# Cross-attention of 64 batches on one core: third q projection moved, residual on ScalarE and GpSimd, value spread reshaped

## What is computed

```python
q = split_heads(x @ w_q)                       # 20 heads of 16
out_text = merge(softmax(q @ k.T / 4) @ v)     # 69 keys
out_ip   = merge(softmax(q @ k_ip.T / 4 + mask) @ v_ip)   # 8 keys
out = (out_text + out_ip) @ w_out + b_out + x  # b_out + x: "the residual"
```

## Time and profile before

| what | us |
|---|---|
| median of 3 runs (1338.42 to 1345.62) | 1341.73 |
| the profiled execution | 1338.48 |
| its span on the core | 1336.7 |
| TensorE busy | 1191.8 (89%) |
| VectorE busy | 1094.9 (82%) |
| ScalarE busy | 833.2 (62%) |
| GpSimd busy | 824.0 (62%) |

### The profile page before, as it was taken

The page is one execution under the profiler, slowest core; times in us unless marked ns, Lnnn a source line. Parts: engine busy times, 40 slices in busy tenths (PEclk is TensorE's granted clock), DMA queues, the critical chain, the costliest instruction groups (busy, mean ns, idle before and its releaser), DMA issues.

```text
span 1336.7 us, 33739 instructions
## 1 busy us (share of the span) xinstructions
PE 1191.8 (89%) x12350; PEld 1113.1 (83%) x12350; DVE 1094.9 (82%) x2438; ACT 833.2 (62%) x1795; POOL 824.0 (62%) x1004
## 2 busy tenths in 40 slices
PE   6998885389999999999999999999999999999986
PEld 5898875278888888888888888888888888888885
DVE  4688876268888888888888888888888888888884
ACT  3343444167777777777667767777777777777761
POOL 0111010057777777777777777777777777777774
PEclk9999998589999999999999999999999999999997
DMA  6388888534444444444444444444454444444431
GB/s 163 68 203 159 182 150 132 97 83 110 110 108 108 108 108 109 109 108 110 107 110 110 111 109 109 108 112 112 110 120 114 112 113 109 108 107 108 97 75 40
DMA packets 361459, 151.26 MB, mean 113 GB/s; under 512 B 298641, under 2 KB 350865, under 8 KB 360017
## 3 DMA queue, kind: packets, MB, share of 16 engines
q1 hardware_dynamic: 361296, 149.13, 50.2%
HBM read 88.17 MB, written 39.90 MB: 96 GB/s over the span
## 4 chain that ended last, share of the span: by engine, by line
DVE 33%; PE 33%; issue 7%; ACT 6%; POOL 1%; DVEq 0%; DMA 0%; POOLq 0%; SPq 0%; ACTq 0%
DVE q_hi_lo L1204 8%; DVE stats L1217 8%; PE ps_a L963 7%; PE ps_b L963 7%; DVE values L1261 6%; PE ps_o L1037 5%; PE ps_m L982 4%; ACT q_hi_lo L1134 4%; DVE y L1251 3%; DVE aT_lo L1238 3%; PE ps_s L1006 3%; PE ps_s L1012 3%; PE ps_a L1055 3%; DVE aT L1240 2%; DVE ip_masked L1214 2%
## 5 line engine op out<-in xcount | busy, mean ns | idle before, releaser
L1318 POOL TENSOR_TENSOR prob_lo<-prob,prob_hi 128x512 f16<-128x512 f32 (+1 forms) x448 | 488.9, 1097 | 181.3 <-ACT prob_hi L1154 174.7
L1153 ACT ACTIVATE prob<-ps_s 128x512 f32<-128x512 f32 (+1 forms) x448 | 254.9, 569 | 249.0 <-PE ps_s L1012 248.6
L1006 PE MATMUL ps_s<-q_hi_lo,keys 128*128 128x256 f32 x960 | 256.5, 304 | 0.0
L1154 ACT ACTIVATE prob_hi<-ps_s 128x512 f16<-128x512 f32 (+1 forms) x448 | 252.3, 563 | 0.0
L1012 PE MATMUL ps_s<-q_hi_extra,keys 128*128 128x256 f32 x960 | 234.4, 281 | 0.7 <-ACT q_hi_extra L1143 0.7
L1217 DVE TENSOR_REDUCE stats<-ps_m 128x8 f32<-128x552 f32 x320 | 230.6, 721 | 0.0
L1327 POOL TENSOR_TENSOR attn<-heads 128x128 f32<-128x128 f32 (+1 forms) x256 | 158.4, 619 | 72.9 <-DVE heads L1231 72.8
L1037 PE MATMUL ps_o<-values,prob_hi 128*128 128x68 f16 (+7 forms) x3328 | 197.2, 195 | 3.6 <-DVE heads L1231 1.9
L1037 PEld LDWEIGHTS ps_o<-values,prob_hi 128*128 128x128 f16 x3328 | 168.5, 98 | 24.3 <-DVE heads L1231 2.2
L1037 PE MATMUL ps_o<-values,prob_lo 128*128 128x68 f16 (+3 forms) x1664 | 188.1, 195 | 0.0
L1012 PEld LDWEIGHTS ps_s<-q_hi_extra,keys 128*128 128x128 f32 x960 | 173.0, 189 | 0.9 <-ACT q_hi_extra L1143 0.9
(11 more groups left out here) (179 smaller groups left out, 3094.9 us busy)
## 6 DMA issues: line engine op xcount, KB each, us to landing
x_in<-in_x_dram SPq DMA_DIRECT2D x64, 320.0 KB, 3.0
q_hi_extra<-q_hi_lo SPq DMA_DIRECT2D x64, 320.0 KB, 3.3
x_keep<-in_x_dram SPq DMA_DIRECT2D x64, 320.0 KB, 4.1
out_dram<-y SPq DMA_DIRECT2D x128, 160.0 KB, 2.9
k_scratch<-k_stage SPq DMA_DIRECT2D x16, 770.0 KB, 5.7
keys<-k_scratch SPq DMA_DIRECT2D x256, 48.1 KB, 2.1
ctx_in<-in_ctx_dram SPq DMA_DIRECT2D x64, 128.0 KB, 2.8
keys<-k_scratch SPq DMA_DIRECT2D x256, 24.1 KB, 1.9
```

What stands on the lines that cost most here:

```text
L1006: mm(ps, keys[:, n, 0, quad, c:c + P], q_hl[n][:, quad, :], start=i == 0, stop=False)
L1153: nc.scalar.activation(prob[:, s, 0:w], ps_s[RING[s]][:, 0:w], ACT.Exp)
L1154: nc.scalar.activation(prob_hi[par(b)][:, s, 0:w], ps_s[RING[s]][:, 0:w], ACT.Exp).then_inc(s_hi, 1)
L1318: nc.gpsimd.tensor_tensor(prob_lo[par(b)][:, s, 0:w], prob[:, s, 0:w], prob_hi[par(b)][:, s, 0:w], ALU.subtract).then_inc(s_lo, 1)
```

## The change

Three things change.

- The third q projection writes `ps_a` instead of `ps_b`. It moves ahead of `stats_transpose`, which now writes `ps_b`. On ScalarE `q_hi(2)` moves ahead of `extra`. On TensorE `max_scores(a,0)` moves ahead of `scores(b,0)`.
- `finish(t)` is split. ScalarE copies the output projection to `y` (`y_out`, ahead of `exps(2)` and `exps(3)`), GpSimd adds `x_keep` in place, both tiles after `rest(4)`. TensorE waits for ScalarE's copies (`s_ye`) before it writes the banks again; the stores wait for GpSimd's (`s_yr`).
- The spread writes four slots of each tile. The fifth slot is used by tiles 1, 6 and 11 alone; one more instruction of 3 x 32 elements, behind the third spread, writes these three.

```diff
+MAIN_SLOTS = 4
+WIDE = [t for t, n in enumerate(NSLOTS) if n > MAIN_SLOTS]
 # SyncE, load_values
-                            sp.wait_ge(s_vx, at(b, 3, 3))
+                            sp.wait_ge(s_vx, at(b, 4, 4))
 # TensorE: x_transpose (attn_transpose: the same change of semaphore)
-                            pe.wait_ge(s_yr, at(b, NT, -3 * NT))
+                            pe.wait_ge(s_ye, at(b, NT, -3 * NT))
 # project
-                            pe.wait_ge(s_qlo, at(b, QUADS, 4))
-                        ps = (ps_a, ps_b, ps_b)[m]
+                            pe.wait_ge(s_qlo, at(b, QUADS, 2))
+                        ps = (ps_a, ps_b, ps_a)[m]
 # stats_transpose
-                            pe.wait_ge(s_qlo, at(b, QUADS, QUADS + 2))
+                            pe.wait_ge(s_qlo, at(b, QUADS, QUADS + 4))
-                            last = nc.tensor.transpose(ps_a[:, t * P:(t + 1) * P], stats[:, t, :], ident[:])
+                            last = nc.tensor.transpose(ps_b[:, t * P:(t + 1) * P], stats[:, t, :], ident[:])
 # TensorE's step
-                        if Bs:
-                            scores(b, 0)
                         if A:
                             max_scores(a, 0)
+                        if Bs:
+                            scores(b, 0)
...
+                        if E:
+                            project(e, 2)
                         if A:
                             stats_transpose(a, E, Ds)
-                        if E:
-                            project(e, 2)
 # ScalarE
+                        def y_out(t):
+                            act.wait_ge(s_op, at(d, NT, t + 1))
+                            if t == 0 and (n is None or n >= 4):
+                                act.wait_ge(s_y[par(d)], nth(d, 32, -32))
+                            nc.scalar.copy(y[par(d)][:, t, :], (ps_a, ps_b)[t][:, 0:D]).then_inc(s_ye, 1)
 # VectorE: finish() and its two calls are gone; in spread_values
-                                .broadcast_to([P, GTILES[g], SLOTS, 2 * DH]),
-                                own_rows[:].rearrange("p t (n c) -> p t n c", n=SLOTS)[:, t], ALU.mult).then_inc(s_vx, 1)
+                                .broadcast_to([P, GTILES[g], MAIN_SLOTS, 2 * DH]),
+                                own[:, t, 0:MAIN_SLOTS, :], ALU.mult).then_inc(s_vx, 1)
+                            if g == 2:
+                                w = slice(WIDE[0], TILES, 5)
+                                nc.vector.tensor_tensor(v[:, w, MAIN_SLOTS, 2:SLOT], raw_v[par(b)][:, w, :],
+                                                        own[:, w, MAIN_SLOTS, :], ALU.mult).then_inc(s_vx, 1)
 # GpSimd
+                        def finish(t):
+                            pool.wait_ge(s_ye, at(d, NT, t + 1))
+                            if t == 0:
+                                pool.wait_ge(s_xb, at(d, 1, 1))
+                            nc.gpsimd.tensor_tensor(y[par(d)][:, t, :], y[par(d)][:, t, :], x_keep[par(d)][:, t, :],
+                                                    ALU.add).then_inc(s_yr, 1)
...
                             rest(3)
                             rest(4)
+                        if Ds:
+                            finish(0)
+                            finish(1)
                         if Cs:
                             add_heads(2)
```

More of the change, by code:

```diff
@@ L89 @@
 SLOTS = max(NSLOTS)
+MAIN_SLOTS = 4
+WIDE = [t for t, n in enumerate(NSLOTS) if n > MAIN_SLOTS]
+assert SLOTS == MAIN_SLOTS + 1 and WIDE == list(range(WIDE[0], TILES, 5))
 VCOLS = TILES * SLOTS * SLOT
@@ L824, in xattn_kernel @@
             s_yr = sem("y_ready")
+            s_ye = sem("y_evacuated")
             s_xk = [sem(f"residual_loaded{q}") for q in range(2)]
@@ L1019, in sum_heads @@
                         if u == 0:
-                            pe.wait_ge(s_vx, at(b, 3, 3))
+                            pe.wait_ge(s_vx, at(b, 4, 4))
                         if t == 0:
@@ L1050, in attn_transpose @@
                         else:
-                            wait(pe, s_yr, b, NT, 0)
+                            wait(pe, s_ye, b, NT, 0)
                         for t in range(NT):
@@ L1068, in step @@
                         e, a, c, d = off(b, 2), off(b, 1), off(b, -1), off(b, -2)
+                        if A:
+                            max_scores(a, 0)
                         if Bs:
                             scores(b, 0)
-                        if A:
-                            max_scores(a, 0)
                         if Cs:
@@ L1139, in a_hi @@
                             nc.scalar.copy(aT2[0:64, :], ps_b[0:64, 0:S]).then_inc(s_ahi, 1)
+                        def y_out(t):
[3 more added lines that the diff above has]
+                            nc.scalar.copy(y[par(d)][:, t, :], (ps_a, ps_b)[t][:, 0:D]).then_inc(s_ye, 1)
                         def extra():
                             act.wait_ge(s_et, at(a, 1, 1))
-                            nc.scalar.copy(q_ex[par(a)][QD:P, 0, :], ps_a[QD:P, 0:S]).then_inc(s_ex, 1)
+                            nc.scalar.copy(q_ex[par(a)][QD:P, 0, :], ps_b[QD:P, 0:S]).then_inc(s_ex, 1)
                             nc.scalar.copy(q_ex[par(a)][QD:P, 1:QUADS, :],
-                                           ps_a[QD:P, 0:S].rearrange("p (o s) -> p o s", o=1).broadcast_to([QD, QUADS - 1, S])
+                                           ps_b[QD:P, 0:S].rearrange("p (o s) -> p o s", o=1).broadcast_to([QD, QUADS - 1, S])
                                            ).then_inc(s_ex, 1)
@@ L1162, in step @@
                             exps(1)
+                        if Ds:
+                            y_out(0)
+                        if Bs:
                             exps(2)
+                        if Ds:
+                            y_out(1)
+                        if Bs:
                             exps(3)
@@ L1174, in step @@
                             exps(6)
+                        if E:
+                            q_hi(2)
                         if A:
                             extra()
-                        if E:
-                            q_hi(2)
                     sched(act, step)
@@ L1241, in a_lo @@
                                                     ALU.subtract).then_inc(s_alo, 1)
[L1243 to L1252, removed]
                         def spread_values(g):
@@ L1312, in step @@
                         E, A, Bs, Cs, Ds = has(n)
-                        a, c = off(b, 1), off(b, -1)
+                        a, c, d = off(b, 1), off(b, -1), off(b, -2)
                         def rest(s):
```

9 lines of the change are left out of this document (3 added, 6 removed).

## The result

The changed kernel takes 1344.32 us (median of 9 runs, 1342.9 to 1347.51), the one before 1339.61 in the runs beside it (9 runs, 1338.42 to 1345.62). The ratio is 1.0034, with a 95% interval of 1.002 to 1.0049. Forecast was 1337.5, a little faster.

A forecast was written before the change was run, and what follows sets the result against it. TensorE's chain with ScalarE and VectorE was taken to bound the 16.34 us step; after the change, GpSimd or `q_lo(2)`. 60 steps x -0.11 = -6.6, edges +3, rounded to -4: 1334.5 profiled, 1337.5 median; range 1324 to 1354.

The forecast's parts named there:

- What bounds the kernel: One 16.34 us step: no engine has much room; the chain runs over TensorE, ScalarE and VectorE, GpSimd not on it.
- X to P: From the start of `attn_transpose` to the next step's `project(e,0)`: 10.10 us, claimed unchanged on this path.
- P to X: From the start of `project(e,0)` to that of `attn_transpose`: 6.24 us, claimed to become 5.9.
- Part 1: Third projection: TensorE's wait before `project(e,2)` goes, a 0.26 wait for `extra` replaces it; -0.34 a step.
- Part 2: Residual: ScalarE's copies at 0.43 each cost nothing, GpSimd's two additions take 1.66 against 1.81 of slack.
- GpSimd's sum: GpSimd's instructions from `rest(2)` through `add_heads(3)`, added up: next `attn_transpose` 16.12 to 16.15 after the last.
- Part 3: Smaller spreads save GpSimd 0.1 a step; the small spread waits for `add_heads(3)` (16.35) or not (16.13); middle 16.23.
- rival 3: The small spread hands the whole gain back: step 16.35, with +3 at the ends 1345; chance 0.23.
- Edges: First and last steps: GpSimd's additions +3.1 in two late steps, very end +0.9, first three steps -1; together +3.
- The signs: Expected in traces: GpSimd without idle from `rest(2)` to `add_heads(3)`, small spread 0.6 if waiting, VectorE -6 points, GpSimd +10.
- Rival 1: GpSimd is not the limit, additions 0.75 each; TensorE's path gives step 16.00, -18 us, 1324; chance 0.15.
- rival 2: Slower by GpSimd alone: additions 0.93 each and the small spread waits; step 16.55, +17 us, 1359; chance 0.20.

## Why the prediction was wrong

Point by point, by its own steps.

- **What bounds the kernel.** Right. From X to P it is 10.10 in the changed kernel too. The part alone that shortens P to X gave 18 us. In every run but two it stays at 10.10 to 10.13; where the small spread held up `maxima(3)` it took 11.40, and with `a_hi` ahead of `exps(0)` 10.60.
- **Part 1** was costed at -0.34 a step and measured -0.23 by itself. The wait for `extra` was forecast at 0.26 with TensorE going on at P + 4.93; the changed kernel shows 0.22 and P + 5.05, the projection alone 0.23 and P + 5.03. That tenth is the miss: from there to X the projection alone takes 0.97, as forecast, and X to P does not change.
- **Part 2** in full steps: right, 0.43 a copy, 0.86 an addition (0.87 forecast), and hidden, by the run with the residual alone.
- **GpSimd's sum.** Right within 0.1: 16.12 to 16.15 forecast, 16.13 in the run with the small spread in the middle. That run does not single it out: `attn_transpose` starts 0.09 after GpSimd's last addition there, and so it does in the projection alone (16.12), where GpSimd has pauses and TensorE's own path sets X. With five slots (16.25) the sum is what is left. Its own prices moved against each other. The second spread ran ahead of `rest(2)`, because VectorE was free earlier, so `rest(2)` took 1.40 and the bias addition 1.56, where I had the delay on the bias.
- **Part 3 is the step that failed.** The two ends were 16.13 and 16.35, by whether the small spread waits for `add_heads(3)`. I took the middle, for which there was no row, though the earlier trace rows showed on VectorE's side that the waiting operation goes before the next one of the engine that runs. Read the other way round it says that GpSimd's waiting instruction goes before VectorE's next. It does: in each run that has a small spread, it ended with the same GpSimd instruction in 61 or 62 of its 64 executions. This was rival 3, put at 0.23, which gave 1345, and 1344.32 was measured. In terms of the sum: 16.23 was taken, 16.40 measured, and 60 times 0.17 is 10 us of the miss in the profiled execution.
- **A waiter was missed.** The small spread raises the count for which `sum_heads(c,0)` waits from 3 to 4. Before, the third spread ended 0.5 before that product was due. I followed `q_lo(2)` alone. Both come within 0.05 of each other in the changed kernel, so the bound of 16.35 was nearly right (16.40), but for half the reason; the run with the small spread last tells them apart.
- **Edges.** +3 was forecast, and +6 was measured in the profiled executions. The two steps counted, 3.1, were 3.5, and 2.9 in the run with the residual alone; the very end, 0.9, was 0.8. The third step was rightly left out for GpSimd; its 2.0 are TensorE's clock, which the sum did not have. The first steps, at -1, gained more: from the first `x_hi` to the first `a_hi` it is 52.23 instead of 56.98, and 50.5 to 52.2 in all runs that move the projection. Only -0.4 is left of it since the first `x_hi` itself came 4.3 later (253.10), in a part that the change does not touch; in kernels that are the same up to there it lies between 250.43 and 253.10. Why the first steps gain 5 and not 1 is not taken apart here.
- **The signs.** GpSimd without a pause and the small spread with 0.6 instead of 0.2 came as written. VectorE's share fell by 4 points instead of 6, since the waiting of the small spread counts as busy, and GpSimd's rose by 8 instead of 10. The last sum of the forecast gives 1337.7 and not 1337.5, which decides nothing.
- Rival 1 did not come, and rival 2 neither: an addition cost 0.83 in a full queue, under its point of decision.

With the mechanism at hand two versions beat both kernels: the projection alone (0.9863), or the whole change with the small spread in the middle and the additions last in the last steps (0.9856). The two cannot be told apart.

## What to carry to other kernels

When an instruction is split or a small one added behind another, look up every semaphore count that it raises, and who waits for it first: the price is that waiter's slack, not the instruction's length. Where two engines exclude each other, a small operation costs what is left of the other engine's instruction that it meets, so place it by the other engine's queue, and check the place again after each other edit. A cost with two ends and no row between them is two cases with a chance each, and its middle is a time that neither gives.

## What the runs showed of the hardware

The exclusion of VectorE's spread and GpSimd's instructions is taken in turns: of two VectorE spreads in a row, the second waits for one whole GpSimd instruction if one is due. 96 elements took 0.32 (behind the 128x64 addition of `add_heads`, 0.32 itself), 0.60 (behind its 128x192 addition, 0.59 alone), 1.18 (behind `rest`, 1.17 alone) and 1.55 (behind the bias addition, 1.55 alone), each the median of 64, and 0.21 at least. The Trainium skill's rule in "SBUF — State Buffer", section "SBUF: two separate sides", that one side blocks the other for a whole instruction, holds in all of these rows. I had not expected that a fifth less work in a spread could cost 5% of a kernel (1393.76 against 1322.73) by moving it into another neighbour's time.

TensorE's granted clock has two levels in these traces. In a stretch at 0.51 of full speed the 16 products of `project_out` took 4.41 us, at 1.00 they took 2.45. Near the end of the execution, where TensorE stands for several microseconds at a time, a run can be at the low level or not in the same step, and 2 us hang on it. So the last steps of two runs can be compared only with the clock beside them.
